# Streaming spilled weights in pairs: twelve loads of 512 KB for a tile instead of twenty-four of 256 KB

## The chip, the cores and the metric

The kernel runs on all 8 cores of one Trainium2 chip. Two cores share one sequence of the batch: each takes the keys and values of the whole sequence and every second token as queries. The metric is the time of one execution in microseconds on the device, that of the slowest core. The cores do not talk to each other.

## The reference

One transformer layer on x of shape (4, 4096, 1024) in float32: causal attention with 16 heads of 64, residual and layer norm; then a feed-forward block whose two linear layers work on quantized data, again residual and layer norm.

```python
x = _layernorm(x + attn(x))                       # causal, 16 heads
h = layernorm(x, ln1_w, ln1_b)
h = bitlinear(h, w1, b1)                          # 1024 -> 4096
h = gelu(h)
h = layernorm(h, ln2_w, ln2_b)
out = bitlinear(h, w2, b2)                        # 4096 -> 1024
x = _layernorm(x + out)

def bitlinear(x, w, b):
    dqx = round(x * 127 / max|x| per token) / scale   # 8-bit values
    dqw = ternary(w / mean|w|) * mean|w|              # -1, 0, 1
    return einsum('btd,hd->bth', dqx, dqw) + b
```

## The kernel before

A core owns 2048 tokens. The kernel has four stages: keys and values of the whole sequence (L464 to L505), attention and output projection by blocks of 512 queries (L546 to L754), the ternary form of both feed-forward weights (L919 to L993), and the feed-forward block on 16 tiles of 128 tokens (L1187 to L1605). A barrier on VectorE (`bar34`) stands before the last stage.

**Where the weights lie.** The ternary second weight has 32 chunks of 128 rows by 1024 columns, in bf16, 256 KB each. Chunks 0 to 7 stay in SBUF. Chunks 8 to 31, the 24 of `w2_streamed`, are written to the scratch tensor `w2spill` in HBM and loaded again for every token tile. Six slots (`NSTSL = 6`) hold them: `wst0` and `wst1` in `wsbuf`, `wst2` to `wst5` in two free places of `kvx` (`WST_EXTRA`), each pair adjacent in steps of 1024 columns. Slot `si % 6` takes the streamed chunk number `si`. The second matmul takes the groups of eight chunks in the order 1, 2, 3, 0, so the streamed ones come first and the resident ones last. All reads of chunk `si` are two matmuls of 512 columns (L1530), one for each half of the output in `ps4` and `ps5`.

**The work of one token tile.** `emit_ffn_front`: first layer norm and quantization on ScalarE and VectorE, transposes on TensorE (L1258), copy to `q1t` (L1265). `emit_ffn_mm1`: eight groups of eight matmuls (L1278) and a bias matmul (L1282) into `ps0` to `ps3`. `emit_ffn_gelu`: GELU (L1301) and squares (L1314) on ScalarE. `emit_ffn_tail`: statistics, second layer norm (L1406, L1414, L1420, maximum at L1426), quantization (L1469 to L1489), for each group eight transposes (L1505), a copy to `q2t` (L1513) and the chunks' matmuls (L1530), the bias (L1542, L1544), eviction into `rbuf` (L1552), last layer norm (L1572 to L1605) and the store. Tiles with even and odd number use two sets of `abuf`, `bbuf`, `h2` and `q1t`, so that the front of tile 6 writes buffers which the tail of tile 4 must have left. `ps4` and `ps5` are used by all tiles in turn.

**Order.** Nothing runs in the order of the program. Every operation is a step with the names that it reads and writes, a planned duration `dur` and, for a DMA, a planned latency `lat`. `Sched.reorder` walks over all steps: it takes the engine whose next ready step can start first, and there, of the steps that could start then, the one of highest rank. The rank is the longest planned way from the step to the end: its duration and latency, plus 0.4 us wherever the next step is on another engine. A DMA without `lat` counts 0.1 us and 2.5 us of latency; with `lat` given it counts 0.12 us and that latency. The order so found is then fixed for each engine, and each engine runs its list strictly in order. Before a step stand waits on semaphores: each engine has one, and each stream slot has one of its own (`dt0` to `dt5`). In the plan of the kernel before, the first matmul of tile 5 starts with rank 327.24, the first streamed chunk of tile 4 has 323.90, the one six later 320.00.

**The loads.** All loads of `w2spill` are issued from GpSimd's queue (POOL). A load into a slot waits for the matmuls that read the slot's last content. Every DMA goes through the helper `dma`, whose issuing line is L412.

Of the kernel before, what the change touches and what calls it, by code (L numbers as in the profile page):

```python
# [185 lines left out]
def build_program(S=4096, dbg=()):  # L186
    E, HID, H, D = 1024, 4096, 16, 64
    NP = H // 2
    TOK = S // 2
    NKB = S // 128  # L190
# [32 lines left out]
    w2sp_d = nc.dram_tensor("w2spill", [HID, E], BF16)  # L223

    dbg_d = {}
    for nm, shape in dbg:
        dbg_d[nm] = nc.dram_tensor("dbg_" + nm, list(shape), F32,
                                   kind="ExternalOutput")
# [7 lines left out]
    kvx = sbat("kvx", [128, NKB * 2048], BF16, KVX_BASE)  # L236
# [36 lines left out]
    WST_EXTRA = []  # L273
# [4 lines left out]
    NSTSL = 2 + len(WST_EXTRA)  # L278
# [64 lines left out]
    wsbuf = sbat("wsbuf", [128, 2 * E], BF16, a.take(2 * E * 2, "wsb"))  # L343
# [33 lines left out]
    w2_streamed = [j for j in range(HC) if w2place[j][0] == "stream"]  # L377
# [9 lines left out]
    def wst_ap(ssl, c0=0, c1=E):  # L387
        if ssl < 2:
            return wsbuf[:, ssl * E + c0: ssl * E + c1]
        off = WST_EXTRA[ssl - 2]  # L390
        return kvx[:, off + c0: off + c1]
# [15 lines left out]
    def dma(eng_name, dst, src, sem, *, reads=(), writes=(), name="",  # L407
            bulk=False, slow=False, lat=None):
        def fn(eng, dst=dst, src=src, slow=slow):
            if slow:  # L410
                return eng.dma_start(dst, src, allow_slow_non_contiguous=True)
            return eng.dma_start(dst, src)  # L412
        return sd.step(eng_name, fn, reads=reads, writes=writes, dma_sem=sem,
                       name=name, bulk=bulk, lat=lat)
# [5 lines left out]
    for t, d, nm in ((ident, ident_d, "identb"), (onesc, onesc_d, "onescb"),  # L420
# [3 lines left out]
            name="ld_" + nm, bulk=True)  # L424
# [3 lines left out]
    for ec in range(EC):  # L428
        dma("gpsimd", qkvw_sb[:, ec * 3 * E:(ec + 1) * 3 * E],
            qkvw_d[ec * 128:(ec + 1) * 128, :], "dw",  # L430
            writes=[f"qkvw{ec}"], name=f"ld_qkvw{ec}", bulk=True, lat=8.0)

    for tg in range(NTG):
# [4 lines left out]
            reads=[f"xkvbf{sl}"], writes=[f"xkvbf{sl}"], name=f"p1ldx{tg}", lat=12.0)  # L438
        for ecn in range(EC):
            bk = ecn % 2  # L440
            def ftr(eng, sl=sl, ecn=ecn, bk=bk):
                r = None
                for t4 in range(4):
# [7 lines left out]
                    reads=[f"xkvbf{sl}", "identb", f"pt{bk}"],  # L451
                    writes=[f"pt{bk}"], name=f"p1xt{tg}_{ecn}", dur=0.9)
            def fev(eng, ecn=ecn, bk=bk):
# [3 lines left out]
                    name=f"p1xe{tg}_{ecn}", dur=0.35)  # L457
# [884 lines left out]
    def emit_ffn_tail(ti):  # L1342
# [6 lines left out]
        cv = C["cv"]  # L1349
        x1r = C["x1r"]  # L1350
        def emit_stream_load(si):
            if si >= len(w2_streamed):
                return
            cc2 = w2_streamed[si]
            ssl2 = si % NSTSL
            dma("gpsimd", wst_ap(ssl2),
                w2sp_d[cc2 * 128:(cc2 + 1) * 128, :], f"dt{ssl2}",
                reads=[f"wst{ssl2}", f"wsp{cc2}"], writes=[f"wst{ssl2}"],
                name=f"f{ti}wl{si}")
        for s5 in range(NSTSL):  # L1360
            emit_stream_load(s5)
        def f2mva(eng):
            eng.tensor_add(cvals[:, Q + 24:Q + 25], cvals[:, Q + 25:Q + 26], cvals[:, Q + 26:Q + 27])
# [135 lines left out]
        for g in gorder:  # L1499
            gb = g % 2  # L1500
            pb = par
            def ftq2(eng, g=g, pb=pb):
                r = None
                for k in range(8):
                    r = eng.transpose(  # L1505
                        pt[pb][:, k * 128:(k + 1) * 128],
                        h2(g * 1024 + k * 128,  g * 1024 + (k + 1) * 128),
                        ident[:, :])
                return r
            sd.step("tensor", ftq2, reads=[HNq[g], "identb", f"pt{pb}"],  # L1510
                    writes=[f"pt{pb}"], name=f"f{ti}t2_{g}", dur=0.9)
            def feq2(eng, gb=gb, pb=pb):
                return eng.tensor_copy(q2t[:, gb * 1024:(gb + 1) * 1024],  # L1513
                                       pt[pb][:, 0:1024])
            sd.step("vector", feq2, reads=[f"pt{pb}", f"q2t{gb}"],
                    writes=[f"q2t{gb}"], name=f"f{ti}e2_{g}", dur=0.6)
            for k in range(8):
                cc = g * 8 + k
                kind = w2place[cc][0]
                if kind == "stream":  # L1520
                    ssl = stream_pos[cc] % NSTSL
                    rres = [f"wst{ssl}"]
                    rhs_ap = lambda c0, c1, ssl=ssl: wst_ap(ssl, c0, c1)
                else:
                    rres = ["w2t"]
                    rhs_ap = lambda c0, c1, cc=cc: w2_home_ap(cc, c0, c1)
                def fmm2(eng, g=g, k=k, gb=gb, cc=cc, rhs_ap=rhs_ap):
                    r = None
                    for nn in range(2):
                        r = eng.matmul(ps[4 + nn][:, 0:512],  # L1530
                                       q2t[:, gb * 1024 + k * 128:
                                              gb * 1024 + (k + 1) * 128],
                                       rhs_ap(nn * 512, (nn + 1) * 512),
                                       start=(cc == cc_first), stop=False)
                    return r
                sd.step("tensor", fmm2,
                        reads=[f"q2t{gb}", "ps4", "ps5"] + rres,
                        writes=["ps4", "ps5"], name=f"f{ti}mm2_{cc}", dur=0.5)
                if kind == "stream":
                    emit_stream_load(stream_pos[cc] + NSTSL)  # L1540
        def fbias2(eng):
            eng.matmul(ps[4][:, 0:512], onesr[0:1, :], b2c[0:1, 0:512],  # L1542
                       start=False, stop=True)
# [176 lines left out]
```

How the kernel before makes its waits and increments, by code:

```python
    def emit(self, eng_name, eng, sems):  # L148
# [7 lines left out]
                if (dep["eng"] == eng_name == "tensor"  # L156
                        and dep["dma_sem"] is None and st["dma_sem"] is None):
                    continue
                key = dep["dma_sem"] if dep["dma_sem"] is not None else dep["eng"]
                assert dep["inc_val"] is not None, \
                    f"{st['name']} deps on {dep['name']} without inc"
                val = self.sem_totals[key] if key in self.bulk_sems else dep["inc_val"]
                waits[key] = max(waits.get(key, 0), val)
            for key in sorted(waits):
                if watermark.get(key, -1) < waits[key]:
                    eng.wait_ge(sems[key], waits[key])
                    watermark[key] = waits[key]
            inst = st["fn"](eng)
            if st["inc_val"] is not None:
                key = st["dma_sem"] if st["dma_sem"] is not None else st["eng"]
                assert inst is not None, f"{st['name']} needs inc, fn returned None"
                inst.then_inc(sems[key], 16 if st["dma_sem"] is not None else 1)
# [1468 lines left out]
        @blk.sync  # L1641
        def _(sync):
            sd.emit("sync", sync, sems)
            for k2 in ("do", "dbg"):
                if k2 in sd.sem_totals:
                    sync.wait_ge(sems[k2], sd.sem_totals[k2])
```

## Time and profile before

| | |
|---|---|
| time, median of 2 runs | 2738.33 us (2720.15 to 2756.52) |
| the profiled execution | 2724.27 us |
| span of its slowest core (core 4) | 2722.7 us |
| spans of the 8 cores | 2676.4 to 2722.7 us |
| mean granted TensorE clock | 0.796 to 0.808 of full speed |
| busy on core 4: PE, DVE, ACT, POOL | 1777.1, 950.7, 1381.5, 254.6 us |
| data moved by DMA | 218.69 MB, mean 80 GB/s |

Spans and rows are of core 4, the slowest. Its profiled time is 1.6 us above its span, and 14 us below the median of the two runs. PE is TensorE, DVE VectorE, ACT ScalarE, POOL GpSimd. In the rows an arrow `<-` between names means "written from"; behind an idle time it names what ended the wait.

### The profile page before, as it was taken

Reading aid. Unit: us, or ns where it says so; the run is one execution under the profiler, and the core shown is the slowest. Engines: PE = TensorE matmul, PEld = TensorE weight load, DVE = VectorE, ACT = ScalarE, POOL = GpSimd, SP = SyncE. Lnnn points to the kernel's source line nnn. Section 1 sums busy time; section 2 is a strip of 40 time slices with the busy share of each in tenths; the row PEclk is TensorE's granted clock in tenths of the full one; section 3 lists DMA queues with packets and bytes.
Section 4 is the critical chain, followed back from the end, with each engine's and each line's share of the span. In section 5 each row is a group of like instructions: output and inputs, shape, how many; then the busy total and the mean of one; then the engine's idle time right before and its main releaser. Section 6 shows DMA issues by size and latency. Waiting matters only on the chain.

```text
span 2722.7 us, 31469 instructions; the slowest of 8 cores (2676.4 to 2722.7 us)
## 1 busy us (share of the span) xinstructions
PE 1777.1 (65%) x9312; PEld 687.7 (25%) x9412; DVE 950.7 (35%) x2196; ACT 1381.5 (51%) x2603; POOL 254.6 (9%) x454
## 2 busy tenths in 40 slices
PE   2999948778757777677674222257566686665766
PEld 1444422222211122222221112122222232222222
DVE  0111100000221011311325556345657555574644
ACT  0222317888548886277161222464655546464553
POOL 1000010000000000000000001203122131221303
PEclk9877979999866788778766555579888787977879
DMA  9011050000074300100102326516233252433415
GB/s 140 16 32 29 3 93 1 1 1 1 16 197 175 124 32 1 47 1 1 47 1 107 110 90 211 117 31 193 77 124 129 80 176 71 148 105 105 151 50 178
DMA packets 63004, 218.69 MB, mean 80 GB/s; under 512 B 12660, under 2 KB 12660, under 8 KB 60533
## 3 DMA queue, kind: packets, MB, share of 16 engines
q0 software_dynamic: 43040, 132.68, 18.4%
q1 hardware_dynamic: 16918, 67.21, 7.2%
q10 hardware_dynamic: 2880, 16.78, 1.7%
q8 instruction: 81, 1.33, 0.2%
q14 instruction: 85, 0.70, 0.1%
HBM read 227.64 MB, written 14.68 MB: 89 GB/s over the span
## 4 chain that ended last, share of the span: by engine, by line
PE 42%; ACT 16%; issue 16%; DVE 15%; DMA 9%; POOL 1%; DVEq 1%; ACTq 0%; SPq 0%; POOLq 0%
PE ps L464 9%; PE ps L1278 9%; ACT ptb L608 6%; PE ps L627 4%; PE ps L586 4%; PE ps L639 3%; ACT ptb L605 3%; PE ps L1530 3%; PE ps L677 3%; DMA kvx<-w2spill 2%; DVE cvx L1426 2%; DVE ternb L933 2%; PE ps L563 2%; DMA onesfb<-onesf 2%; DMA wstA<-w 2%
## 5 line engine op out<-in xcount | busy, mean ns | idle before, releaser
L605 ACT ACTIVATE ptb<-ps 128x512 bf16<-128x512 f32 (+7 forms) x640 | 336.2, 525 | 138.1 <-PE ps L643 104.0
L608 ACT ACTIVATE ptb<-ps 128x512 bf16<-128x512 f32 (+7 forms) x640 | 334.7, 523 | 0.0
L586 PE MATMUL ps<-QT,kvx 64*128 64x512 bf16 (+7 forms) x640 | 246.3, 385 | 131.7 <-ACT ptb L608 119.2
L627 PE MATMUL ps<-ptb,onescb 128*64 128x512 bf16 (+7 forms) x640 | 259.1, 405 | 20.2 <-DVE ptb L619 10.4
L639 PE MATMUL ps<-ptb,kvx 128*64 128x512 bf16 (+7 forms) x640 | 253.6, 396 | 27.3 <-DVE attnT L663 27.3
L1278 PE MATMUL ps<-kvx,q1t 128*128 128x512 bf16 x1007 | 263.8, 406 | 10.8 <-DVE q1t L1265 6.6
L464 PE MATMUL ps<-xT,qkvw_sb 128*128 128x512 bf16 x996 | 261.7, 419 | 9.5 <-DVE xT L454 7.2
L1530 PE MATMUL ps<-kvx,q2t 128*128 128x512 bf16 x739 | 211.3, 418 | 86.0 <-DMA kvx<-w2spill 40.7
L631 PE MATMUL ps<-ptb,onescb 128*64 128x512 bf16 (+7 forms) x640 | 265.4, 415 | 0.0
L616 DVE TENSOR_TENSOR ptb<-ptb,dmaskb 128x64 bf16<-128x64 bf16 x256 | 49.1, 192 | 594.8 <-ACT ptb L608 592.8
L643 PE MATMUL ps<-ptb,kvx 128*64 128x512 bf16 (+7 forms) x640 | 255.0, 398 | 0.0
L589 PE MATMUL ps<-QT,kvx 64*128 64x512 bf16 (+7 forms) x640 | 253.1, 395 | 0.0
L950 PE MATMUL pt<-identb,ternb 128*128 128x128 bf16 x512 | 64.1, 306 | 201.5 <-ACT kvx L993 130.0
L586 PEld LDWEIGHTS ps<-QT,kvx 64*128 64x128 bf16 x640 | 60.5, 94 | 413.1 <-issue 410.3
L412 POOL DMA_DIRECT2D kvx<-w2spill x256 | 137.8, 539 | 164.6 <-PE ps L1530 116.6
L1258 PE MATMUL pt<-identb,abuf 128*128 128x128 bf16 x128 | 13.4, 268 | 195.9 <-DVE cvals L1452 151.5
L464 PEld LDWEIGHTS ps<-xT,qkvw_sb 128*128 128x128 bf16 x1024 | 105.1, 106 | 137.1 <-issue 85.0
L1278 PEld LDWEIGHTS ps<-kvx,q1t 128*128 128x128 bf16 x1024 | 96.6, 102 | 144.0 <-issue 59.3
L993 ACT ACTIVATE kvx<-pt 128x128 bf16<-128x128 bf16 x160 | 44.2, 277 | 164.3 <-DVE kvx L989 164.2
L412 POOL DMA_DIRECT2D wsbuf<-w2spill x128 | 70.1, 548 | 577.8 <-PE ps L1530 566.0
L1530 PEld LDWEIGHTS ps<-kvx,q2t 128*128 128x128 bf16 x768 | 70.5, 104 | 211.5 <-issue 169.5
L627 PEld LDWEIGHTS ps<-ptb,onescb 128*64 128x64 bf16 x640 | 71.3, 111 | 176.9 <-issue 174.0
(166 smaller groups left out, 2751.7 us busy)
## 6 DMA issues: line engine op xcount, KB each, us to landing
kvx<-w2spill POOLq DMA_DIRECT2D x256, 256.0 KB, 4.3
wsbuf<-w2spill POOLq DMA_DIRECT2D x128, 256.0 KB, 3.9
wstA<-w SPq DMA_DIRECT2D x32, 512.0 KB, 5.3
wstA<-w SPq DMA_DIRECT2D x8, 2048.0 KB, 7.8
xkvbf<-xkv POOLq DMA_DIRECT2D x8, 1024.0 KB, 10.2
xres<-xq SPq DMA_DIRECT2D x16, 512.0 KB, 3.4
wbuf<-w ACTq DMA_DIRECT2D x16, 512.0 KB, 3.8
wbuf<-w SPq DMA_DIRECT2D x16, 512.0 KB, 3.6
```

Of the source, the lines that this page charges most:

```text
L412: return eng.dma_start(dst, src)
L464: r = eng.matmul(ps[bk][:, 0:512], qkvw_sb[:, ec * 3 * E + typ * E + p * 128: ec * 3 * E + typ * E + (p + 1) * 128], xT1[:, ec * 512:(ec + ...
L586: eng.matmul(ps[sA][:, noff:512], kt_ap(kb, p, 0, 64), QT[0:64, p * 512 + noff:(p + 1) * 512], start=True, stop=True, tile_position=(0, 0))
L589: return eng.matmul(ps[sB][:, noff:512], kt_ap(kb, p, 64, 128), QT[64:128, p * 512 + noff:(p + 1) * 512], start=True, stop=True, tile_posi ...
L605: eng.activation(ptb[:, ptA + noff: ptA + 512], ps[sA][:, noff:512], AF.Exp, bias=cSH, scale=c0125)
L608: return eng.activation(ptb[:, ptB + noff: ptB + 512], ps[sB][:, noff:512], AF.Exp, bias=cSH, scale=c0125)
L627: eng.matmul(ps[5][0:64, noff:512], onesc[:, :], ptb[:, ptA + noff: ptA + 512], start=(kb == 0), stop=(kb == nkb - 1), tile_position=(0, 0 ...
L631: return eng.matmul(ps[5][64:128, noff:512], onesc[:, :], ptb[:, ptB + noff: ptB + 512], start=(kb == 0), stop=(kb == nkb - 1), tile_posit ...
L639: eng.matmul(ps[4][0:64, noff:512], v_ap(kb, 2 * p), ptb[:, ptA + noff: ptA + 512], start=(kb == 0), stop=(kb == nkb - 1), tile_position=( ...
L643: return eng.matmul(ps[4][64:128, noff:512], v_ap(kb, 2 * p + 1), ptb[:, ptB + noff: ptB + 512], start=(kb == 0), stop=(kb == nkb - 1), ti ...
L1278: eng.matmul(ps[pn][:, 0:512], q1t[:, pq + k * 128: pq + (k + 1) * 128], w1t_ap(k, c0, c0 + 512), start=(k == 0), stop=False)
L1530: r = eng.matmul(ps[4 + nn][:, 0:512], q2t[:, gb * 1024 + k * 128: gb * 1024 + (k + 1) * 128], rhs_ap(nn * 512, (nn + 1) * 512), start=(cc ...
```

## The change

The load of one chunk becomes the load of two. `emit_stream_load` does nothing for odd numbers; for an even number it issues one DMA with two pieces of 2 KB for each of the 128 partitions, into the slots `si % 6` and the next one, and waits for the readers of both. The second half of the pair is no longer issued by itself, and only the semaphores `dt0`, `dt2` and `dt4` are used. At the start of a tile's tail three pairs are asked for instead of six chunks. After that a pair is asked for behind the matmuls of every odd streamed chunk, and it takes the slots of that chunk and the one before. The planned latency of a load becomes 5.0 us (with 0.12 us of issue) where it was 2.5 (with 0.1). Slots, their number, the bytes loaded and all arithmetic stay.

```diff
--- before.py
+++ after.py
@@ -1349,15 +1349,25 @@
         cv = C["cv"]
         x1r = C["x1r"]
         def emit_stream_load(si):
-            if si >= len(w2_streamed):
+            if si % 2 or si >= len(w2_streamed):
                 return
             cc2 = w2_streamed[si]
             ssl2 = si % NSTSL
-            dma("gpsimd", wst_ap(ssl2),
-                w2sp_d[cc2 * 128:(cc2 + 1) * 128, :], f"dt{ssl2}",
-                reads=[f"wst{ssl2}", f"wsp{cc2}"], writes=[f"wst{ssl2}"],
-                name=f"f{ti}wl{si}")
-        for s5 in range(NSTSL):
+            if ssl2 < 2:
+                dstap = bass.AP(wsbuf, 0, [[2 * E, 128], [E, 2], [1, E]])
+            else:
+                o0 = WST_EXTRA[ssl2 - 2]
+                dstap = bass.AP(kvx, o0, [[NKB * 2048, 128],
+                                          [WST_EXTRA[ssl2 - 1] - o0, 2],
+                                          [1, E]])
+            srcap = bass.AP(w2sp_d, cc2 * 128 * E,
+                            [[E, 128], [128 * E, 2], [1, E]])
+            dma("gpsimd", dstap, srcap, f"dt{ssl2}",
+                reads=[f"wst{ssl2}", f"wst{ssl2 + 1}",
+                       f"wsp{cc2}", f"wsp{cc2 + 1}"],
+                writes=[f"wst{ssl2}", f"wst{ssl2 + 1}"],
+                name=f"f{ti}wl{si}", lat=5.0)
+        for s5 in range(0, NSTSL, 2):
             emit_stream_load(s5)
         def f2mva(eng):
             eng.tensor_add(cvals[:, Q + 24:Q + 25], cvals[:, Q + 25:Q + 26], cvals[:, Q + 26:Q + 27])
@@ -1536,8 +1546,8 @@
                 sd.step("tensor", fmm2,
                         reads=[f"q2t{gb}", "ps4", "ps5"] + rres,
                         writes=["ps4", "ps5"], name=f"f{ti}mm2_{cc}", dur=0.5)
-                if kind == "stream":
-                    emit_stream_load(stream_pos[cc] + NSTSL)
+                if kind == "stream" and stream_pos[cc] % 2 == 1:
+                    emit_stream_load(stream_pos[cc] - 1 + NSTSL)
         def fbias2(eng):
             eng.matmul(ps[4][:, 0:512], onesr[0:1, :], b2c[0:1, 0:512],
                        start=False, stop=True)
```

## Rows read from the trace of the kernel before

**Rows 1.** The page, part 1: busy time, share of the span, instructions of each engine.

```profile
PE 1777.1 (65%) x9312; PEld 687.7 (25%) x9412; DVE 950.7 (35%) x2196; ACT 1381.5 (51%) x2603; POOL 254.6 (9%) x454
```

**Rows 2.** Busy time by stretch: PE, PEld, DVE, ACT, POOL, granted clock, DMA share, GB/s.

```profile
1965.00:2080.00 115.00, 76.36 (x347) 29.64 (x351) 66.31 (x125) 62.27 (x95) 25.90 (x48) 0.85 0.36 119
...
2195.00:2310.00 115.00, 77.70 (x343) 30.45 (x348) 66.46 (x124) 62.18 (x95) 25.32 (x47) 0.83 0.36 117
```

**Rows 3.** The chain that ended last, 1830 to 2722 us, shares of that stretch.

```profile
by line: PE ps L1278 24.8%; issue 17.1%; PE ps L1530 8.1%; DMA kvx<-w2spill 7.0%; DVE cvx L1426 5.7%; PE ps L1282 4.2%; DVE bbuf L1482 3.2%; ACT abuf L1406 3.0%; DVE kvx L1489 2.0%; DVE bbuf L1414 1.8%; PE pt L1505 1.7%; ACT L1387 1.4%; ACT
```

**Rows 4.** Waits of PE, 1840 to 2722 us: total us, times, longest.

```profile
PE pt L1258 <- DVE cvals L1452: 151.5, 7, 21.9
PE ps L1530 <- DMA kvx<-w2spill: 40.7, 44, 2.6
PE ps L1530 <- DVE rbuf L1552: 23.4, 8, 3.2
...
PE ps L1530 <- DMA wsbuf<-w2spill: 11.6, 19, 2.1
```

**Rows 5.** Instructions that touch w2spill: idle time before them, time to landing.

```profile
  PE ps L1530: 682.5, 119
...
DMA to landing us min/median/max: 2.8/4.1/20.3
```

**Rows 6.** Timeline of PE, 2160 to 2280 us: start, us, line, operation, idle before.

```profile
2166.21 3.38 PE L1278 MATMUL ps<-kvx,q1t 128*128 128x512 bf16 x8 [0.94 <-DVE q1t L1265]
...
2176.30 0.62 PE L1505 MATMUL pt<-identb,h2b 128*128 128x128 bf16 x8
...
2178.89 1.04 PE L1530 MATMUL ps<-wsbuf,q2t 128*128 128x512 bf16 x4
...
2185.89 0.38 PE L1282 MATMUL ps<-b1c,onesrb 1*128 1x512 bf16 x1
...
2192.22 2.34 PE L1530 MATMUL ps<-kvx,q2t 128*128 128x512 bf16 x6 [0.34 <-DMA kvx<-w2spill]
...
2215.05 1.01 PE L1530 MATMUL ps<-wsbuf,q2t 128*128 128x512 bf16 x2 [2.89 <-DVE rbuf L1552]
...
2232.68 0.59 PE L1530 MATMUL ps<-kvx,q2t 128*128 128x512 bf16 x2 [0.40 <-DMA kvx<-w2spill]
...
2243.24 2.54 PE L1530 MATMUL ps<-kvx,q2t 128*128 128x512 bf16 x11
...
2253.88 0.38 PE L1282 MATMUL ps<-b1c,onesrb 1*128 1x512 bf16 x1
...
2279.09 1.01 PE L1258 MATMUL pt<-identb,abuf 128*128 128x128 bf16 x8 [21.59 <-DVE cvals L1452]
```

**Rows 7.** Timeline of POOL, 2160 to 2230 us.

```profile
2226.01 0.54 POOL L412 DMA_DIRECT2D kvx<-w2spill  x1 [2.31 <-PE ps L1530]
2226.87 0.54 POOL L412 DMA_DIRECT2D kvx<-w2spill  x1 [0.31 <-issue]
```

**Rows 8.** Timeline of DVE, 2155 to 2235 us.

```profile
2168.06 1.23 DVE L1489 SCALAR_TENSOR_TENSOR h2b<-abuf,bbuf 128x1024 bf16<-128x1024 bf16 x1
...
2230.66 0.67 DVE L1265 COPY q1t<-pt 128x1024 bf16<-128x1024 bf16 x1
```

**Rows 9.** Groups of POOL's instructions: busy us, mean ns, idle before.

```profile
L412 POOL DMA_DIRECT2D w2spill<-wstage x24 | 22.1, 920 | 395.0 <-ACT kvx L993 352.0 <-ACT wstage L961 33.7 <-DMA w2spill<-wstage 7.8
L412 POOL DMA_DIRECT2D xkvbf<-xkv x8 | 6.2, 772 | 254.1 <-PE pt L444 253.2 <-POOLq L198 0.9
```

**Rows 10.** The page, parts 3 and 6, and one stretch of the busy times.

```profile
q0 software_dynamic: 43040, 132.68, 18.4%
...
xkvbf<-xkv POOLq DMA_DIRECT2D x8, 1024.0 KB, 10.2
xres<-xq SPq DMA_DIRECT2D x16, 512.0 KB, 3.4
...
2187.00:2212.00 25.00, 19.20 (x91) 7.57 (x89) 17.49 (x34) 14.70 (x19) 11.82 (x22) 0.86 0.70 231
```

## The prediction

> **What bounds the kernel now.** I read, in this order: the busy times of the page, the engines by stage, the chain of work that ended last, TensorE's waits, the loads of the spilled weights, and one pair of token tiles instruction by instruction. The page has TensorE at 65% of the span and no other engine above 51% [rows 1], so no engine is full. The change acts only on the loads of `w2spill`, which run in the last stage, from about 1830 to 2722 us. The table by stage shows a steady pattern there: every 115 us the kernel does two token tiles, with TensorE busy 76 to 78 us, VectorE 66, ScalarE 62 and the DMA engines at 0.36 [rows 2]. A stage in which nothing is full is bound by latency: the path goes first matmul (L1278, L1282), GELU, the second layer norm, quantization, transposes (L1505), second matmul (L1530), eviction, front of the tile after next, and again first matmul.
>
> In the chain of that stage the streamed weights appear as 7.0% of 892 us, so 62 us [rows 3]; one passage costs a landing of about 4.2 us, so there are some 15 passages in 16 tiles, about two in each pair. TensorE itself stood 40.7 us for the loads into `kvx` and 11.6 us for those into `wsbuf`, 52.3 us in all, against 151.5 us for VectorE in front of the next tile's transposes and 23.4 us for the eviction [rows 4]. So 52 us, 1.9% of the span, is the whole that perfect streaming could hand back directly. A load lands 4.1 us after its issue (median) and the shortest wanted 2.8 [rows 5].
>
> **Which waits end last in one pair of tiles.** Call the tiles 4, 5 and 6, and the streamed chunks of one tile c0 to c23. The first matmul of tile 5 starts at 2166.2 and ends at 2186.3. Transposes of tile 4 stand at 2176.3, c0 and c1 at 2178.9. The other chunks of tile 4 come as a burst behind the first matmul, with a wait for a load at 2192.2, and end about 2212. Tile 5's own chunks start at 2215.05, after 2.89 us for the eviction of tile 4, and c17, again after a load, stands at 2232.7; the first matmul of tile 6 follows and ends at 2254.3, and TensorE then idles 21.6 us until 2279.1 [rows 6]. Each of the two bursts meets the loads once on the path. In the second, c14 is issued at 2226.0 and c15 0.86 us later, although POOL works only 0.54 us for one [rows 7]: it follows the pace at which TensorE frees the slots. The operand of tile 6's first matmul, `q1t`, is done at 2231.3, two microseconds before that matmul starts [rows 8].
>
> **The change, part by part.**
>
> *Fewer issues.* 384 loads of 256 KB become 192 of 512 KB. POOL is busy 0.54 us for one [rows 7]. Nothing in the trace shows a copy of two pieces of 2 KB for each partition. The cast load of four pieces for each partition took 0.77 us and the store of eight short pieces 0.92 [rows 9]; I take 0.60, with bounds 0.54 and 0.92. That is 208 us of POOL work down to 115 (104 to 177), none of it on the path by itself: POOL stands idle 682 us waiting for L1530 [rows 5]. Value 0; at most the pieces of POOL in the chain, about 0.5 us a passage, 15 passages, 8 us.
>
> *Longer landing.* In the burst from 2187 to 2212 the queues moved 231 GB/s [rows 10]; 256 KB more are then 262144 / 231000 = 1.13 us. All of the software queue's data over its share of the span gives 132.68 MB / (0.184 x 2722.7 us) = 265 GB/s, which is 0.99 us [rows 10]. The bounds are 0 (the 512 KB load on SP's queue lands in 3.4 us, less than our 256 KB) and (10.2 - 4.1) / 3 = 2.0 us for each further 256 KB, from the 1024 KB load that casts [rows 10]. I take +1.0, so a pair lands in 5.1 us.
> The Trainium skill (DMA: Bandwidth & Descriptors, "Anatomy of one DMA") puts a DMA at a fixed 2.0 us and the bytes over 436 GB/s; by that the second half would add an estimated 0.6 us and a pair would land in 3.2. This trace's median of 4.1 for 256 KB is above its 2.6. By it the sum below would be 3 us lower.
>
> *Coarser release.* A pair is issued only when its second chunk is used, one chunk (two matmuls, 0.46 us: 11 matmuls took 2.54 us at 2243 [rows 6]) after the first half could have been; the slots are 3 instead of 6 but hold the same bytes. Where a passage is exposed as now, it grows by 1.0 + 0.46 = 1.5 us (0.46 to 2.5). Behind the waiting issue on POOL stand only further loads, and for them waits TensorE, with the next first matmul queued behind c17.
>
> *The planner's cost.* `lat=5.0` makes the planner believe in 0.12 + 5.0 us for a load, where it believed in 0.1 + 2.5 and the trace had 4.1. One turn from a chunk over the release and the load to the chunk six later was 0.5 + 0.4 + 2.6 + 0.4 = 3.9 planned us, and becomes 0.5 + 0.5 + 0.4 + 5.12 + 0.4 = 6.9. Three turns lie in a tile, so c0 of a tile rises by 9 planned us, c6 by 6, c12 by 3, the rest by 0. Before, c0 of tile 4 stood 3.3 below the first matmul of tile 5 (323.9 against 327.2); it will stand 5.7 above. So the transposes and c0 to c5 should go in front of most of tile 5's first matmul, since group 1 of tile 4 is quantized by 2169.3 [rows 8] and its transposes wait until 2176.3 merely because of the order. The later pairs then land while the first matmul runs. In the second burst the first matmul of tile 6 overtakes c12 to c17: it starts when `q1t` is ready (2231.3) and not after c17 (2233.1).
> What this is worth: the waits for loads shrink, I estimate by half of 52.3, which is 26 us. The first matmul of tile 5 ends later by up to 16 chunks and two transposes in front of it, 16 x 0.46 + 2 x 0.6 = 8.6 us, and the second matmul of tile 4 ends earlier by about as much (2212 to 2203). The two meet: tile 5's layer norm starts later, tile 6's front can start earlier, and VectorE is busy for both. I take these as cancelling, with 8 pairs x 8.6 = 69 us as the bound on either side. All steps before the last stage keep their order but for ties, since every path passes the barrier ahead of it.
>
> *Sum.* Against the profiled execution (2724.3 us, span 2722.7): -26 for hidden waits, +11 for the 7 or 8 passages left at 1.5 us, +4.5 for the last tile, whose three reloads have no first matmul to hide behind, 0 for POOL. That is -10, so 2714 where the profiled run stood at 2724, and 2728 from the median of 2738. The two runs span 36 us, so I put the new time between the two: 2720 us.
>
> **The rivals.**
> 1. *The order hardly changes, only the landing grows.* For it: ranks choose only among steps that are ready, and tile 4's groups become ready one by one. Then all 15 passages cost 1.5 us and the last tile 4.5: +27, so 2751 on the profiled run and up to 2765 on the median.
> 2. *Clearly slower: the first matmul is displaced.* Place: 2166 to 2186. Tile 5's first matmul ends 8.6 us later, and with it GELU, layer norm and tile 5's quantization, while tile 4's earlier end buys nothing. It decides if the chain after the change leaves L1278 into L1301 and L1406 in each odd tile with TensorE's wait before L1505 grown. Price 8 x 8.6 = 69, less 10, gives 2783 to 2790. Against it: tile 5's second matmul waits now for the eviction of tile 4 (2.89 us) as well, so both ends are close.
> 3. *Clearly faster: streaming hidden and eviction early.* All 52.3 us of load waits and the 23.4 us for `rbuf` vanish, +4.5 for the last tile: -71, 2653 us. For it: the plan's latency now fits the measured one. Against: TensorE's 151.5 us before L1258 belong to VectorE's order and stay.
> The Trainium skill (DMA: Bandwidth & Descriptors, "Rules for kernel authors") says to coalesce small transfers into large ones. That speaks for this side; the trace has POOL idle and the DMA engines at 0.36, so here it would have little to work on.
> 4. *Nothing measurable*: POOL's issues were never on the path and the extra landing lies under idle time; 2724 to 2738, inside my forecast.
>
> **Numbers.** My case (with 4) 0.50, rival 1 0.20, rival 2 0.14, rival 3 0.16. The likeliest alone would lie in 2700 to 2745. The range must reach towards both clear rivals, since 69 us either way is the bound of the re-planned order: 2660 to 2785. A measurement of this kernel tells about 2%, 55 us, from no change: faster by more 0.17, same 0.68, slower by more 0.15.
>
> **What would show it.** In the profile after: 192 loads of 512 KB, POOL about 0.6 us each, landing near 5.1 (0 and 2.0 above 4.1 are the bounds). TensorE's waits for `w2spill` near 26 us; 50 or more means rival 1. In the pair of tiles, L1505 and the first L1530 stand inside the first L1278 block, and no load wait stands in front of the even tile's L1278. The period of 115 us should stay within 2 us; 106 is rival 3, 124 rival 2. What would make me wrong first is the cancellation in the re-planned order, which I argued from one pair of tiles: each microsecond a pair that does not cancel is 8 us of time.

## The result and the profile after

The changed kernel is slower: median 2789.36 us over 11 runs (2761.02 to 2834.63) against 2726.28 us over 10 runs of the kernel before. The ratio is 1.020, 95% interval 1.014 to 1.026. A second set of runs of the same kernel gave 1.021 (1.016 to 1.027). The medians are of all runs, while the ratios leave out the executions in which the cores of one die ran slower at a lower granted clock; the profiled execution of the first set was one of those, so the profile shown here is of the second (`e12_changed_again`, 2778.94 us). Line numbers behind L1349 are higher by 10 than in the kernel before: L1530 is now L1540, L1505 is L1515.

The page (slowest core, core 5) holds what the diff promises: half the loads, twice the size, the same bytes (132.66 MB against 132.68 [rows 10]). POOL falls from 254.6 to 183.1 us; the other engines' busy time hardly moves [rows 1].

```profile
PE 1800.8 (65%) x9412; PEld 701.8 (25%) x9412; DVE 956.8 (34%) x2196; ACT 1390.2 (50%) x2603; POOL 183.1 (7%) x262
...
q0 software_dynamic: 39968, 132.66, 17.5%
...
kvx<-w2spill POOLq DMA_DIRECT2D x128, 512.0 KB, 5.1
wsbuf<-w2spill POOLq DMA_DIRECT2D x64, 512.0 KB, 3.9
```

All that follows is core 4, as in the rows of before. Two token tiles now take 124 us where they took 115 [rows 2]. The engines do the same work in it, at a lower granted clock (0.81 against 0.83 to 0.85):

```profile
1990.00:2114.00 124.00, 80.22 (x354) 32.79 (x357) 67.43 (x125) 62.78 (x95) 16.59 (x24) 0.81 0.32 111
2114.00:2238.00 124.00, 80.87 (x353) 33.05 (x357) 67.99 (x125) 63.31 (x95) 17.50 (x25) 0.81 0.33 112
```

The chain that ended last, 1850 to 2772 us, tells where they went. The loads fell from 7.0% of 892 us (62 us) [rows 3] to 1.8% of 922 us (17 us), better than forecast. VectorE's layer norm and quantization took their place: `bbuf` at L1492 and L1424 (before L1482 and L1414) rose from 3.2% + 1.8% = 45 us to 5.0% + 4.2% = 85 us.

```profile
by line: PE ps L1278 23.0%; issue 14.4%; PE ps L1540 8.6%; DVE cvx L1436 5.4%; DVE bbuf L1492 5.0%; DVE bbuf L1424 4.2%; PE ps L1282 3.9%; ACT ubuf L1479 3.2%; ACT abuf L1486 2.3%; ACT L1397 1.9%; ACT abuf L1416 1.9%; DMA kvx<-w2spill 1.8%;
```

TensorE's waits in that stretch (total us, times, longest) changed their kind. The 151.5 us before the front's transposes L1258 [rows 4] are gone; instead TensorE waits 113.4 us for quantized data (`h2b`) and 60.8 us for `cvals` in front of L1515. For the loads it stands 35.7 + 21.2 = 56.9 us, no less than the 52.3 of before, yet the chain no longer runs through most of them.

```profile
PE pt L1515 <- DVE h2b L1499: 113.4, 14, 15.7
PE pt L1515 <- DVE cvals L1575: 60.8, 7, 9.8
PE ps L1540 <- DVE q2t L1523: 40.6, 14, 3.5
PE ps L1540 <- DMA kvx<-w2spill: 35.7, 21, 3.2
PE ps L1540 <- DMA wsbuf<-w2spill: 21.2, 9, 2.7
```

**One passage from an even to an odd tile.** TensorE's timeline (start, us, operation, idle before) of the changed kernel:

```profile
2246.26 1.67 PE L1278 MATMUL ps<-kvx,q1t 128*128 128x512 bf16 x7 [0.28 <-issue]
...
2264.64 0.38 PE L1282 MATMUL ps<-b1c,onesrb 1*128 1x512 bf16 x1
...
2270.80 6.04 PE L1540 MATMUL ps<-kvx,q2t 128*128 128x512 bf16 x19 [3.08 <-DMA kvx<-w2spill]
...
2277.01 0.37 PE L1554 MATMUL ps<-b2c,onesrb 1*128 1x512 bf16 x1
2291.59 1.01 PE L1515 MATMUL pt<-identb,h2b 128*128 128x128 bf16 x8 [14.21 <-DVE h2b L1499]
...
2297.40 3.62 PE L1540 MATMUL ps<-kvx,q2t 128*128 128x512 bf16 x8
...
2306.16 3.19 PE L1278 MATMUL ps<-kvx,q1t 128*128 128x512 bf16 x7 [1.57 <-DVE q1t L1265]
...
2317.98 1.89 PE L1540 MATMUL ps<-kvx,q2t 128*128 128x512 bf16 x8
```

and VectorE's beside it:

```profile
2273.18 0.69 DVE L1424 TENSOR_TENSOR bbuf<-abuf,ln2w_r 128x1024 bf16<-128x1024 bf16 x1 [1.44 <-ACT abuf L1416]
...
2278.78 4.59 DVE L1436 TENSOR_REDUCE cvx<-h2b 128x1 f32<-128x1024 bf16 x4
...
2283.86 0.75 DVE L1562 SCALAR_TENSOR_TENSOR rbuf<-ps,cvals,kvx 128x512 f32<-128x512 f32 x1
...
2291.36 0.68 DVE L1192 TENSOR_TENSOR bbuf<-abuf,ln1w_r 128x1024 bf16<-128x1024 bf16 x1
...
2301.22 1.28 DVE L1492 SCALAR_TENSOR_TENSOR bbuf<-h2b,cvals,abuf 128x1024 bf16<-128x1024 bf16 x1
...
2304.95 0.69 DVE L1265 COPY q1t<-pt 128x1024 bf16<-128x1024 bf16 x1
```

The even tile's first matmul starts at 2246.3, the odd one's at 2306.2: 59.9 us. The same passage of the kernel before took 48.0 us (from 2233.1 to 2281.05); its VectorE:

```profile
2258.45 0.75 DVE L1552 SCALAR_TENSOR_TENSOR rbuf<-ps,cvals,kvx 128x512 f32<-128x512 f32 x1
...
2262.83 0.69 DVE L1192 TENSOR_TENSOR bbuf<-abuf,ln1w_r 128x1024 bf16<-128x1024 bf16 x1 [0.52 <-ACT abuf L1187]
...
2265.56 1.28 DVE L1414 TENSOR_TENSOR bbuf<-abuf,ln2w_r 128x1024 bf16<-128x1024 bf16 x2
...
2272.20 4.59 DVE L1426 TENSOR_REDUCE cvx<-h2b 128x1 f32<-128x1024 bf16 x4
...
2280.21 0.69 DVE L1265 COPY q1t<-pt 128x1024 bf16<-128x1024 bf16 x1
```

Before, VectorE evicted the odd tile (L1552), began the front of the next odd tile (L1192) 8.6 us after the even tile's first matmul ended (2254.3), and laced the even tile's second layer norm (L1414) into it. Now the even tile's whole second layer norm, its maxima and the first quantization stand ahead of the front, and L1192 starts 26.3 us after the end of that matmul (2265.0). Front to odd first matmul got shorter (14.8 against 18.2 us; laced into it are now three more groups of the even tile's quantization, as the L1492 at 2301.22, and no longer its layer norm and maxima), and the even first matmul too (18.8 against 21.2). The sum is 17.8 - 3.4 - 2.4 = +12.0, the 11.9 us between the two intervals but for rounding. The load wait before 2270.80 lies beside VectorE's work and costs nothing: the second matmul that it delays ends at 2277.4 (L1554), and VectorE comes to evict its result (L1562) only at 2283.86.

**The measure used below.** The last stage starts at 1707 to 1790 us, differing with core and run, though the order of work ahead of it is the same in all kernels. So beside the ratio I give the length of the last stage (from the start of the last store into `w2spill` to the core's end, median of 8 cores) and the two intervals of a pair of tiles, between the starts of the first matmuls: even to odd, odd to even (core 2, a typical value). The first two tiles are left out of the intervals: their first matmuls start 18 to 19 us apart in every kernel, so that seven passages of each kind remain.

| kernel | ratio to before (95%) | last stage, us | even to odd / odd to even |
|---|---|---|---|
| before | | 966.4 | 48.0 / 67.0 |
| changed | 1.020 (1.014 to 1.026) | 1036.7 | 59.9 / 64.9 |
| changed, again (`e12`) | 1.021 (1.016 to 1.027) | 1037.2 | 59.9 / 64.6 |
| `e1` pairs, old order | 1.009 (1.005 to 1.012) | 997.7 | 48.0 / 70.8 |
| `e2` singles, new order | 1.027 (1.020 to 1.033) | 1034.7 | 59.8 / 64.8 |
| `e3` singles, `lat=5.0` | 1.016 (1.011 to 1.022) | 1021.7 | 57.1 / 65.8 |
| `e4` pairs, `lat=2.5` | 1.011 (1.006 to 1.015) | 1004.1 | 50.2 / 70.0 |
| `e5` new even-to-odd passage | 1.036 (1.027 to 1.044) | 1070.3 | 61.8 / 68.0 |
| `e6` old even-to-odd passage | no ratio; 2765.65 and 2770.89 us, before 2716.69 | 1023.0 | 50.6 / 71.5 |
| `e7` TensorE's overtaking alone | 1.001 (0.997 to 1.005) | 974.7 | 50.6 / 66.3 |
| `e8` front behind layer norm | 1.029 (1.017 to 1.040) | 1043.7 | 58.8 / 67.5 |
| `e9` fronts late, singles | 0.981 (0.975 to 0.987) | 918.5 | 19.0 / 90 |
| `e10` fronts early, singles | 1.008 (1.004 to 1.012) | 990.6 | 45.0 / 74 |
| `e11` fronts late, pairs | 0.999 (0.994 to 1.004) | 966.6 | 19.0 / 95.5 |
| `e13` late release, old order | two runs, no ratio | 980.6 | 48.0 / 68.0 |
| `e14` late release, order of `e9` | two runs, no ratio | 940.4 | 18.8 / 91.5 |

The changed kernel's account closes: 7 even-to-odd passages at +11.9 are +83, 7 odd-to-even at -2.1 are -15, together +68; the stage is 70 us longer and the medians differ by 63.

### The profile page after: what moved, and what is told of

Same layout as the page of the kernel before. It is cut to its first block, busy times and chain, and to the rows that moved or that the text cites. A ratio compares the mean times of both kernels' runs of the same rounds, so it can differ in the third digit from the quotient of the medians.

```text
span 2808.9 us, 30772 instructions; the slowest of 8 cores (2749.0 to 2808.9 us)
## 1 busy us (share of the span) xinstructions
PE 1840.7 (66%) x9412; PEld 713.6 (25%) x9412; DVE 956.2 (34%) x2196; ACT 1386.8 (49%) x2603; POOL 183.7 (7%) x262
## 3 DMA queue, kind: packets, MB, share of 16 engines
q0 software_dynamic: 39968, 132.66, 18.0%
## 4 chain that ended last, share of the span: by engine, by line
PE 42%; ACT 17%; DVE 17%; issue 14%; DMA 8%; DVEq 1%; ACTq 0%; POOL 0%; SPq 0%; POOLq 0%
PE ps L464 10%; PE ps L1278 8%; ACT ptb L608 6%; PE ps L627 4%; PE ps L586 4%; PE ps L639 3%; PE ps L1540 3%; PE ps L677 3%; ACT ptb L605 3%; DVE cvx L1436 2%; DMA w2spill<-wstage 2%; DMA wstA<-w 2%; PE ps L563 2%; DVE bbuf L1492 2%; DVE ternb L933 2%
## 5 line engine op out<-in xcount | busy, mean ns | idle before, releaser
L464 PE MATMUL ps<-xT,qkvw_sb 128*128 128x512 bf16 x1024 | 283.2, 440 | 6.1 <-DVE xT L454 5.9
L627 PE MATMUL ps<-ptb,onescb 128*64 128x512 bf16 (+7 forms) x640 | 260.7, 407 | 21.0 <-DVE ptb L619 10.8
L1540 PE MATMUL ps<-kvx,q2t 128*128 128x512 bf16 x768 | 234.2, 462 | 31.8 <-DMA kvx<-w2spill 31.8
L589 PE MATMUL ps<-QT,kvx 64*128 64x512 bf16 (+7 forms) x640 | 254.6, 398 | 0.0
L1540 PE MATMUL ps<-wsbuf,q2t 128*128 128x512 bf16 x256 | 88.2, 480 | 71.1 <-DVE q2t L1523 40.5
L1540 PEld LDWEIGHTS ps<-kvx,q2t 128*128 128x128 bf16 x768 | 86.6, 116 | 169.6 <-issue 119.9
L505 DVE COPY kvx<-pt 128x512 bf16<-128x512 bf16 x64 | 27.2, 425 | 266.6 <-PE pt L496 266.6
L486 ACT ACTIVATE vtmp<-ps,qkvb_s 128x512 bf16<-128x512 f32 x64 | 44.0, 687 | 148.0 <-PE pt L496 90.5
```

Source lines behind the costliest of these rows:

```text
L464: r = eng.matmul(ps[bk][:, 0:512], qkvw_sb[:, ec * 3 * E + typ * E + p * 128: ec * 3 * E + typ * E + (p + 1) * 128], xT1[:, ec * 512:(ec + ...
L589: return eng.matmul(ps[sB][:, noff:512], kt_ap(kb, p, 64, 128), QT[64:128, p * 512 + noff:(p + 1) * 512], start=True, stop=True, tile_posi ...
L627: eng.matmul(ps[5][0:64, noff:512], onesc[:, :], ptb[:, ptA + noff: ptA + 512], start=(kb == 0), stop=(kb == nkb - 1), tile_position=(0, 0 ...
L1540: r = eng.matmul(ps[4 + nn][:, 0:512], q2t[:, gb * 1024 + k * 128: gb * 1024 + (k + 1) * 128], rhs_ap(nn * 512, (nn + 1) * 512), start=(cc ...
```

## The experiments

The diffs in this section are shortened to what they do; words in them stand for tables and patterns that the kernels spell out.

**1. Size of the loads or order of the work.** The order of every engine's list can be taken from the plan of another kernel. `e1` loads in pairs with the lists of the kernel before, `e2` loads single chunks with the lists of the changed kernel:

```diff
+PAIR_RUN, ENG_PLAN = True,  {every engine: plan of (single, lat 2.5)}   # e1
+PAIR_RUN, ENG_PLAN = False, {every engine: plan of (pairs, lat 5.0)}    # e2
```

> Loads in pairs, but every engine runs its list in exactly the order of the kernel before (a pair stands in the queue where its second half stood). Theory A, the planner's new order costs the time: the pairs alone cost what I priced, 0 to 1.5 us at each of 15 passages, so 2726 to 2750 us, period of two tiles 115 to 118 us. Theory B, the pair itself costs (longer landing, later release, three slots instead of six): about the time of the changed kernel, 2780 us, with TensorE's waits for the loads well above 55 us.

> The opposite: 24 single loads for each tile as before, every engine in exactly the order of the changed kernel. Theory A: 2765 to 2785 us with a period of about 123 us, since the order is what costs. Theory B: near the kernel before, 2726 us.

Four corners of the last stage: 966, 998 (`e1`), 1035 (`e2`), 1037. The new order costs 68 us with single chunks and 39 with pairs; pairs cost 31 us in the old order and 2 in the new. `e2` has not one changed load and all of the loss. In the old order the pairs lie bare on the path; TensorE's waits and the chain's shares of `e1` (core 4, 1850 to 2737 us for the waits, 1830 to 2722 us for the chain) show it:

```profile
PE pt L1262 <- DVE cvals L1476: 151.5, 7, 21.9
PE ps L1554 <- DMA kvx<-w2spill: 96.8, 58, 3.8
...
PE ps L1554 <- DMA wsbuf<-w2spill: 16.4, 11, 1.9
```

```profile
by line: PE ps L1282 24.4%; DMA kvx<-w2spill 16.2%; PE ps L1554 13.9%; issue 13.3%; DVE cvx L1450 4.4%; PE ps L1286 4.1%; ACT abuf L1430 2.2%; DVE bbuf L1506 1.6%; ACT ubuf L1493 1.6%; DVE bbuf L1438 1.4%; ACT abuf L1500 1.3%; PE pt L1529 1
```

The wait of 151.5 us is untouched to the decimal [rows 4], and the load waits are 113 us, twice those of before.

**2. Which edit makes the order: the pairing or `lat`.** The planner is left to order by itself:

```diff
-                name=f"f{ti}wl{si}")
+                name=f"f{ti}wl{si}", lat=5.0)      # e3, single chunks
-                name=f"f{ti}wl{si}", lat=5.0)
+                name=f"f{ti}wl{si}", lat=2.5)      # e4, pairs
```

> The kernel before with one number changed, the planned latency of a streamed load, 5.0 for 2.5; single loads, planner left free. Theory A, in the form that the larger number alone turns the ranks round: slower by 1 to 3%, 2755 to 2800 us, and VectorE runs the second layer norm of a tile ahead of the next tile's front. Theory B: 2726 us within 1%, as nothing that the chip does is changed but the order.

> The changed kernel with the planned latency put back to 2.5; pairs, planner left free. One turn of the stream is then 0.5 + 0.5 + 0.4 + 2.62 + 0.4 = 4.4 planned us against 3.9 before and 6.9 in the changed kernel. Theory A: most of the loss comes back, 2720 to 2750 us. Theory B: stays near 2780 us.

`lat=5.0` alone lengthens the stage by 55 us and stretches the even-to-odd passage to 57.1; pairs with 2.5 stay near `e1` (38 against 31). So the number in the plan is most of the cause (55 of 68 us), and the loads on the chip none of it: three turns with 5.12 for 2.6 planned us raise c0 by 7.6 planned us, and the other 1.5 of the 9 come from the later release of a pair in the plan.

The planner, run on both kernels, gives the ranks behind this. Against the first matmul of tile 5 the first VectorE step of tile 5's front (L1192) stands 9.26 planned us higher in both plans. The first one of tile 4's second layer norm (L1414, now L1424) stood 7.74 higher before and stands 16.80 higher now: it was below the front and has passed it, by the same 9.06 planned us as the chunks c0 to c5.

**3. Which part of the order.** `e7` puts only TensorE's steps of the odd-to-even passage (first matmul of the even tile, second matmul and transposes of the odd one) in the new order. `e8` leaves TensorE alone and moves the front of the next odd tile behind the even tile's second layer norm on VectorE and ScalarE, with the eviction first:

```diff
+SUBSET = {"tensor": [first matmul of t, second matmul and transposes of t-1]}    # e7
+vector: evict t-1, layer norm 2 of t, maxima of t, quantize one group of t,     # e8
+        front of t+1 (L1192 ...), ...
```

> Single loads, order of the kernel before, but on TensorE alone, in the passage from an odd to an even tile, the first matmul of the even tile overtakes chunks 12 to 17 of the odd tile, as in the changed kernel. In the forecast this part was worth -2 us at the start of the first matmul and +1 at the end of the second, so about nothing. Theory A1: the last stage 955 to 975 us. Theory A3, the late end of the odd tile's second matmul (30.8 us behind the start of the first matmul in the changed kernel, 24.2 before) is what makes the next front late, whatever VectorE's order: 990 us or more.

> Single loads, TensorE exactly as in the kernel before. On VectorE and ScalarE alone, the front of the odd tile is put behind the even tile's second layer norm and its first quantized group, instead of among them; the eviction stays where it was. Theory A1 in its narrow form (VectorE's order is enough): the first matmul of the odd tile starts 6 to 8 us later, so the last stage is 1005 to 1025 us. If TensorE's order (six chunks and two transposes of the even tile ahead of the first matmul) is the larger part, below 990.

`e7` costs 8 us of stage and nothing that the whole time can tell: on TensorE the earlier first matmul of the even tile and the later second matmul of the odd one nearly cancel in this passage. `e8` costs 77 us and stretches the even-to-odd passage by 10.8 us, 7 x 10.8 = 76. More than I had expected, since the odd-to-even side gives nothing back here. In its waits (core 4, 1850 to 2760 us) the 151.5 us have grown into

```profile
PE pt L1263 <- DVE abuf L1254: 227.8, 8, 32.7
PE ps L1555 <- DMA kvx<-w2spill: 33.1, 35, 2.7
```

The waits for the loads hardly moved: over the whole stage they are 48.6 us on core 4 (before 52.4), and 49 us as the median of the 8 cores (before 48). In `e2`, where TensorE's list is new as well, that median is 37. So the front's place costs the time, and the shorter load waits come only where TensorE's list changes too. That the eviction comes first in `e8` shows that not its place but the front's decides.

**4. The passage both ways.** `e5` puts all of the even-to-odd passage (VectorE, ScalarE, and TensorE's steps of the odd tile's first and even tile's second matmul) in the new order on the old lists; `e6` does the opposite on the new lists.

```diff
+OTHER, base = plan(pairs, lat 5.0), plan(single)     # e5
+OTHER, base = plan(single), plan(pairs, lat 5.0)     # e6
+for each even tile: steps of SUBSET, among themselves, in the order of OTHER
```

> Single loads, order of the kernel before, except at the passage from an even tile to the odd one behind it (seven of them): there VectorE, ScalarE and TensorE take the order of the changed kernel, with the eviction of the odd tile and the front of the next odd tile behind the even tile's second layer norm, and the even tile's transposes and first six chunks ahead of the odd tile's first matmul. Theory A1, this passage is the loss (in the changed kernel the first matmul of the odd tile starts 59.9 us after that of the even tile, before 48.0; the other passage gained 3.1): the last stage grows by 7 x 9 to 7 x 12 us, 1030 to 1050 us against 966, the whole to 2775 to 2795 us. Theory A2, the loss comes from the passage from odd to even, where the first matmul overtakes streamed chunks: the last stage stays within 10 us of 966.

> The opposite: single loads, order of the changed kernel, except that the seven passages from an even to an odd tile have the order of the kernel before. Theory A1: the last stage comes back from 1035 to 966 or less; if the gain of 3.1 us in the other passage is real, to about 945, and the whole to 2680 to 2705 us, faster than the kernel before. Theory A2: the last stage stays near 1035.

`e5` is worse than the changed kernel (+104 us of stage): the passage takes 61.8 and the other interval, which keeps its old order, grows a little as well. `e6` is a miss: I had expected 945 us of stage. It did bring the passage back to 50.6, but the other interval went to 71.5, and the stage lost only 12 to 14 us against the changed kernel. In the new order the even tile's second matmul begins ahead of the odd tile's first (the L1540 at 2297.40 above); put back, those chunks have to be made up behind, which would lengthen the other interval, but no run separates this. So the passage as the place is shown by `e5` and `e8`; that its old order could simply be put back is refuted.

**5. The other direction: fronts later or earlier than in the kernel before.** If 9 planned us in favour of the chunks cost this much, what do 9 us on the fronts themselves do? In `e11` the planned latency is 1.98 us, so that a turn of the pairs is planned as long as one of the single chunks, and every engine has the order of `e9`.

```diff
-                return (rank[j] - pen, -j)
+                bon = BONUS if re.fullmatch(FRONT_STEPS, name) else 0.0
+                return (rank[j] - pen + bon, -j)   # e9: -9, e10: +5, e11: -9 and pairs
```

> Search for a faster order. Single loads, the kernel before, with 9.0 taken from the rank of every front step (first layer norm, quantization, transposes, copy to q1t). The planner then arrives at another pattern: the second matmul of a tile is run to its end before the next tile's first matmul, and the first matmuls of two tiles stand one behind the other. If two first matmuls in a row cover VectorE's work of the other tile, the pair of tiles takes less than 115 us and the last stage less than 966 us. If the stream, which then has no first matmul to land under, is the bound, its waits on TensorE grow from 52 to over 120 us and the stage is longer than 966.

> Single loads, the kernel before, with 5.0 added to the rank of every front step: VectorE does the odd tile's front further ahead among the even tile's second layer norm. By e8, where the front behind it cost 10.8 us a passage, moving it forward should gain: the start of the odd tile's first matmul comes 2 to 4 us earlier (44 to 46 us behind that of the even tile instead of 48.0), the last stage 940 to 955 us, the whole 1% faster. If the even tile's layer norm, pushed back by as much, then sets the next passage, the sum of both intervals stays 115 us.

> The order of the run before the last one (front ranks less 9.0), with loads in pairs. Theory A, pairs cost only where a burst of chunks is not covered by a first matmul: this order has whole second matmuls in one burst, so pairs cost here at least what they cost in the order of the kernel before, 31 us in the last stage, up to 3 turns x 1.5 us x 16 tiles = 72 us. If pairs are cheap here too, their cost in that order had another cause.

`e9` beats both kernels: 2679.16 us against 2720.21, 0.981 (0.975 to 0.987). With fronts late enough those of an even and an odd tile come together, and so do their first matmuls. TensorE's timeline (core 2; L1285 is the first matmul, L1557 the second):

```profile
1969.62 1.89 PE L1285 MATMUL ps<-kvx,q1t 128*128 128x512 bf16 x8
...
1986.81 0.62 PE L1265 MATMUL pt<-identb,abuf 128*128 128x128 bf16 x8
1988.59 1.67 PE L1285 MATMUL ps<-kvx,q1t 128*128 128x512 bf16 x7 [1.16 <-ACT h2b L1308]
```

19.0 us from one first matmul to the next, 90 back to the even one: 109 for the pair instead of 115, at a granted clock of 0.88. The gain does not come from the loads; TensorE waits longer for them (76.2 against 48.9 us on this core):

```profile
1959.00:2068.00 109.00, 81.31 (x353) 32.46 (x361) 68.42 (x124) 62.07 (x94) 26.47 (x49) 0.88 0.40 131
```

```profile
PE ps L1557 <- DMA kvx<-w2spill: 59.3, 54, 4.0
...
PE ps L1557 <- DMA wsbuf<-w2spill: 16.9, 19, 1.7
```

What vanished is the 151.5 us before the front's transposes. `e10` missed: fronts 5 planned us earlier shorten the even-to-odd interval to 45.0 as expected, but the next one grows by 7, and the stage is 24 us longer, where I had expected 11 to 26 less. Pairs on top of `e9` (`e11`) cost 48 us of stage and give all of the gain back; in its chain (core 4, 1830 to 2722 us) the loads head the list:

```profile
by line: DMA kvx<-w2spill 22.7%; PE ps L1557 19.4%; PE ps L1285 13.6%; issue 10.6%; DVE bbuf L1509 3.4%; DVE bbuf L1441 2.6%; DVE cvx L1453 2.6%; ACT abuf L1503 2.6%; PE ps L1289 2.3%; ACT abuf L1433 2.0%; ACT ubuf L1496 1.7%; DVE h2b L1447
```

**6. What in a pair costs.** `e13` (old order) and `e14` (order of `e9`) keep loads of 256 KB, but the load into an even slot also waits until the odd slot's chunk is used, as a pair must.

```diff
-reads=[f"wst{ssl2}", f"wsp{cc2}"]
+reads=[f"wst{ssl2}", f"wsp{cc2}", f"use{ssl2 + 1}"]   # even slots only
```

> 24 single loads for a tile and every engine in the order of the kernel before; only, the load into an even slot waits also for the chunk in the odd slot beside it, as a pair does. It parts the cost of a pair (31 us in the last stage: 998 against 966) into release and landing. If the later release is the cost: 985 to 998 us. If the landing of one 512 KB load is (4.7 us against 4.2, and the first chunk waits for both halves): 966 to 975 us. By my price of 0.46 of 1.5 us for the release: about 975.

> The same late release with single loads in the order of the faster kernel (front ranks less 9.0), where the pairs cost 48 us (966.6 against 918.5). Release: 945 to 967 us. Landing: 918 to 930 us. By the same share, 0.46 of 1.5: 933.

The late release alone costs 14 of the 31 us in the old order and 22 of the 48 in the other; both lie between the two theories. Each is read from one profiled execution. `e14` is the less sure: its cores spread from 931 to 952 us, and the four whose granted clock in this stage matches that of `e9` (0.86 to 0.87) take 931 to 939 us, which would be 16 of the 48. The rest, 17 and 26 us (or 32), is left for the landing as one transfer; it is a remainder, not a measurement of its own. The repeat of the changed kernel ran beside `e9` to `e11`:

> The changed kernel again, beside the others on one chip. The stages add up: last stage 1035 to 1039 us, 2770 us in all, 2 to 2.7% above the kernel before; the same as single loads in its order (1035 us) within 3 us.

## Why the prediction was wrong

I forecast 2720 us, in a range of 2660 to 2785, and no measurable change; it is 2 to 2.3% slower, with a median of 2789.

**The step that failed** is *The planner's cost*. Its arithmetic on the ranks held (c0 stands 5.72 planned us above the first matmul of tile 5, where it stood 3.34 below), and on TensorE things went as said (transposes and c0 to c5 of the even tile in front of the odd tile's first matmul, the even tile's first matmul starting with `q1t`). But I gave the 9 us only to TensorE's steps. A rank is the longest way to the end, so every step on the way to c0 rises with it: the even tile's second layer norm, maxima and quantization on VectorE and ScalarE. They were weighed anew against the front of the next odd tile, and passed it. The prediction held that the 151.5 us before L1258 "belong to VectorE's order and stay"; VectorE's order is what changed. The front starts 17.8 us later behind the even first matmul, +11.9 us a passage net, +83 us in seven. `e2` and `e8` show this with no change to the loads.

**I take these as cancelling** was said of TensorE in the even-to-odd passage: the odd tile's first matmul later, the even tile's second one earlier. No run has that alone. `e7` tests the other passage, where the even tile's first matmul overtakes c12 to c17, and there it gives +8 us. `e5` has the even-to-odd displacement together with VectorE's and ScalarE's and stands 27 us of stage above `e8`, which has no change on TensorE; since the two also differ in VectorE's list, that is a sign against a full cancellation and no measurement of it. In the passage shown above the odd tile's first matmul waits for VectorE and not for the chunks in front of it. The step that the forecast failed on for certain is the one above: VectorE's order was held to be fixed.

**The load waits.** Forecast: halved, 26 of 52.3 us returned. Measured: 56.9 us of waits, but 17 us instead of 62 in the chain. For single chunks the new order shortens the waits from 48 to 37 us (medians of the cores, `e2`), so by 11 and not by half. Against pairs in the old order (113 us of waits) it does halve them, and there it is worth 29 us (pairs cost 31 in the old order, 2 in the new). That this is close to my 26 is luck: the 26 were half of the waits of the kernel before. It came with a loss of 68 us.

**Longer landing and coarser release.** The old-order terms were +27 in sum (rival 1); `e1` has +31 in the stage and +24 in the medians. Inside the sum both parts were off. With the order held the landing grew by 0.6 to 0.9 us, not by 1.0: from 4.1 to 4.7 in the old order (`e1`), from 3.9 to 4.8 in the new one (`e2` to changed), from 4.3 to 4.9 in that of `e9` (`e11`; medians on core 4). By the figures of the Trainium skill (DMA: Bandwidth & Descriptors, "Anatomy of one DMA") the added bytes are an estimated 0.6 us and a pair lands in 3.2: the traces agree with the difference at their lower end, and not with the absolute time. The late release is worth 14 us (`e13`), where 15 passages of 0.46 us made 7.

**Fewer issues.** A pair costs POOL 0.716 us, not 0.60, inside the bounds of 0.54 and 0.92. POOL stayed off the path (1% of the chain that ended last before, 0% after): it sat idle 819 us waiting for L1540. Instructions that touch `w2spill` in the changed kernel, core 4 (min/median/max ns; idle before; landing, the 24 stores among them):

```profile
L412 POOL DMA_DIRECT2D kvx<-w2spill x128: 704/716/783, 1740.4 to 2751.7; - x128
L412 POOL DMA_DIRECT2D wsbuf<-w2spill x64: 704/716/1087, 1739.7 to 2746.1; - x64
...
  PE ps L1540: 819.4, 133
...
DMA to landing us min/median/max: 3.2/4.8/19.7
```

**The rivals.** Rival 2 named the right time (2783 to 2790), as its sign a period of 124 us, and the matmul that comes late, the odd tile's first one; it did not name what makes it late, and that its number fits is luck. It had that matmul pushed back by the even tile's chunks on TensorE. Those do stand in front of it, but at 2306.16 it starts behind a further wait of 1.57 us for `q1t`, from the front that VectorE now begins 17.8 us later. Of its deciding signs, TensorE's wait before L1505 (now L1515) did grow, to 113.4 + 60.8 us; but L1406 (now L1416) fell from 3.0 to 1.9% of the chain, and the odd-to-even interval behind the displaced matmul became shorter, 67.0 to 64.9. Rival 3 fell: most of the loads did leave the chain, and the kernel was slower all the same. The Trainium skill (DMA: Bandwidth & Descriptors, "Rules for kernel authors") says to coalesce many small transfers and calls those under 64 KB mostly overhead; loads of 256 KB are above that, and this case gives no support for joining them. With the order held, loads twice the size cost 31 us (`e1`) and 48 us (`e11` against `e9`), since in a ring of slots a pair's load starts later (`e13`) and lands later, and nothing in the trace was short of issues or bandwidth. Rival 4 fell with the ratio. That the order of all work before the last stage stays was right. One reading was loose: the idle time of 21.6 us before 2279.1 begins at 2257.5, behind the rest of tile 5's second matmul, and not at the end of the first matmul at 2254.3.

**What stays open.** The remainder of a pair's cost (17 and 26 us) was not measured by itself. Nor was TensorE's share in the even-to-odd passage. And I can't say why the odd-to-even interval grows in `e6` by more than the overtaking accounts for in `e7`.

## What to carry to other kernels

In a kernel ordered by a static planner, a duration or latency is part of the ranking of everything upstream of it, on every engine. Before changing one, list which steps on every engine rise with it and what each will now pass; to measure an edit, hold the order fixed and change the edit alone, then the reverse. And a plan fitted better to the measured latency is no better plan: here the gain lay in shifting the fronts (-48 us of stage, `e9`), which no wait for a load pointed to.

## What the runs showed of the hardware

- A load of two pieces of 2 KB for each partition costs POOL 0.716 us of issue, one piece 0.54, and the landing grows by only 0.6 to 0.9 us with the second 256 KB, from medians of 3.9 to 4.3 us.
- TensorE pays for its idle time again behind it. Eight matmuls of L1540 took 3.62 us at 2297.40, soon after an idle time of 14.2 us, at a granted clock of 0.50 (the level of 1.2 GHz), and 1.89 us at 2317.98, in the middle of unbroken work, at 1.00 (2.4 GHz). The kernel with the fewest gaps had the highest clock (`e9` 0.88, before 0.83 to 0.85, changed 0.81), so a change of order is paid or rewarded a second time.
- Cores of one run enter the last stage up to 38 us apart though they have done the same work in the same order (before: core 7 at 1711 us, core 4 at 1749), while their last stages agree within 12 us. The later ones show the lower mean granted clock (0.796 on core 4, 0.807 on core 7).
